# Sparse graph attention: when the neighbour rows of the first two lists of irregular rows are gathered, and when they are mixed

## The chip, the cores and the metric

The kernel runs on 1 core of one Trainium2 chip. The metric is device time in microseconds (us). Before the change three runs had a median of 823.53 us (822.4 to 824.62). A difference of about 0.3% (2.5 us) is the least that a measurement of this kernel can tell from none.

## The reference, cut to what matters

```python
h = jnp.maximum(_layernorm(x, axis=-1), 0.0)          # x: 8192 x 128
s_i = h @ attn[:d]; s_j = h @ attn[d:]
e = jax.nn.leaky_relu(s_i + s_j.T, negative_slope=0.2) # 8192 x 8192
e = e + jnp.where(adj > 0, 0.0, -1e9)                  # adj: 8192 x 8192 int32, 1 entry in 2048 set
out = x + jax.nn.softmax(e, axis=1) @ h
```

Each row of adj has some four neighbours on average. The kernel finds them and handles a row by its own few neighbours only.

## The kernel before, in words

adj is 8192 rows by 8192 int32, 268 MB, and all of it is read once. A tile is 128 rows (one in each partition); there are 64 tiles and so 32 pairs. One step p of 0 to 31 handles the pair of tiles 2p and 2p+1, in four halves of 128 x 4096 int32 (2 MB each):

- **SP** (the queue that loads and stores) issues the four halves of step p (`load_pair`, L413) into `adj_ring`, which has five places. A half may be issued when ACT has signed the half five before it. Between the loads of two steps SP stores a finished pair (`store_pair`, L418): after `load_pair(p)` it waits for the sum of pair p-4 (`pair_mixed`).
- **ACT** turns each half into signs (`sign_tile`, L610). In each step it also does a small exponential for a pair (`exp_pair`, L627, between the first two halves), and in the steps of `DEEP_MIX` one more, `exp_m` (L631), between the third and the fourth half.
- **PE** packs the signs into words (L1364) and collects irregular rows (`list_pair`, L1390).
- **DVE** takes maxima of the words (`max_tile`, L766), finds from them up to eight neighbour numbers of each row (`find_pair`, which ends in `near_id`, L818), scores the gathered neighbours of pair p-2 (`score_pair`, L903 to L919) and adds them up with their weights (L952).
- **POOL** gathers: 12 indirect DMAs for each pair (`gather_pair`, L518), each 128 rows of 528 bytes out of `h_table`. It waits for `near_id` of the pair.

Rows that don't fit that form are collected over the eight steps of a segment (`SEG` = 8) into a list of up to 128 rows; there are four lists, m = 0 to 3. List m is complete at step 8(m+1), where DVE finds 16 neighbour numbers for each of its rows (`find_deep`, which ends in `id_m`). POOL then gathers them with 16 indirect DMAs (`gather_m`, L529) and one for the rows of x (L534) into `near_m` and `x_m`, which have one copy each. `DEEP_PARTS` says how many of the 16 go behind the gathers of a pair in each step, and `DEEP_MIX` in which step of the segment the list is mixed: DVE waits for all 16 gathers (`score_deep`, L1015 to L1026), ACT does `exp_m`, DVE adds up (`add_deep`, to L1052), and POOL stores the result with an indirect DMA (`store_m`, L543), which stands ahead of that step's `gather_pair`. The last list is gathered and mixed behind the loop, and that is the same in both kernels.

The order on each engine is that of the code; nothing else reorders it. In the text S(p) is the time at which ACT starts to sign the first half of step p.

Of the kernel before, what the change touches and what calls it, by code (L numbers as in the profile page):

```python
# [5 lines left out]
def graph_attention_kernel(nc: bass.Bass, x: bass.AP, adj: bass.AP, attn: bass.AP, out: bass.AP):  # L6
# [46 lines left out]
    SEG = 8  # L53
# [3 lines left out]
    CLOSING = 3  # L57
    BODY = PAIRS - CLOSING

    DEEP_PARTS = (4, 4, 4, 4)  # L60
    DEEP_MIX = 6
    FAR = float(2 * N)
    MASKED = -1.0e9
    NOTHING = -1.0e30
# [36 lines left out]
    with ctx:  # L101
# [343 lines left out]
        def _(pool):  # L445
# [67 lines left out]
            def gather_pair(p):  # L513
                pool.wait_ge(near_id_ready, p + 1)
                if p >= RING:
                    pool.wait_ge(pair_mixed, p - RING + 1)
                for k in range(SLOTS):
                    pool.indirect_dma_start(  # L518
                        out=near[:, p % RING, k, :], out_offset=None, in_=table,
                        in_offset=bass.IndirectOffsetOnAxis(ap=near_id[:, p % IDS, k:k + 1], axis=0),  # L520
                        bounds_check=last_code, oob_is_err=False).then_inc(near_in[p % RING], 16)

            def gather_m(m, slots):
                if slots[0] == 0:
                    pool.wait_ge(id_m_ready, m + 1)
                    if m > 0:
                        pool.wait_ge(mixed_m_ready, m)
                for k in slots:
                    pool.indirect_dma_start(  # L529
                        out=near_m[:, k, :], out_offset=None, in_=table,  # L530
                        in_offset=bass.IndirectOffsetOnAxis(ap=id_m[:, k:k + 1], axis=0),
                        bounds_check=last_code, oob_is_err=False).then_inc(near_m_in, 16)
                if slots[-1] == DEEP - 1:
                    pool.indirect_dma_start(  # L534
                        out=x_m[:, :], out_offset=None, in_=x,
                        in_offset=bass.IndirectOffsetOnAxis(ap=row_m[:, m % 2:m % 2 + 1], axis=0),
                        bounds_check=last_row, oob_is_err=False).then_inc(x_m_in, 16)

            def store_m(m):
                pool.wait_ge(mixed_m_ready, m + 1)  # L540
                for e in range(2):
                    pool.wait_ge(stored[e], 16 * (m + 1) * SEG // 2)
                pool.indirect_dma_start(  # L543
                    out=out, out_offset=bass.IndirectOffsetOnAxis(ap=row_m[:, m % 2:m % 2 + 1], axis=0),
                    in_=mixed_m[:, 0, :], in_offset=None,
                    bounds_check=last_row, oob_is_err=False).then_inc(stored_m, 16)

            def load_lone(b):
                pool.wait_ge(lone_id_ready[b], 1)
                pool.indirect_dma_start(  # L550
                    out=lone_x[b], out_offset=None, in_=x,
                    in_offset=bass.IndirectOffsetOnAxis(ap=lone_id[b][:, 0:1], axis=0),
                    bounds_check=last_row, oob_is_err=False).then_inc(lone_x_in[b], 16)
# [8 lines left out]
                    bounds_check=last_row, oob_is_err=False).then_inc(lone_stored[b], 16)  # L562

            for p in range(PAIRS):
                if p >= SEG and p % SEG == DEEP_MIX:
                    store_m(p // SEG - 1)
                gather_pair(p)
                if p == FIRST_STEP + 2:
                    load_lone(0)
                m = p // SEG - 1  # L570
                if m >= 0 and p % SEG < len(DEEP_PARTS):
                    at = sum(DEEP_PARTS[:p % SEG])
                    gather_m(m, range(at, at + DEEP_PARTS[p % SEG]))
            gather_m(SEGS - 1, range(0, DEEP))
            load_lone(LAST)
            store_lone(0)
# [23 lines left out]
        def _(act):  # L600
            act.wait_ge(consts, 1)

            def sign_tile(t, halves=(0, 1)):
                for h in halves:
                    n = 2 * t + h
                    act.wait_ge(adj_in[n % HALVES], 16 * (n // HALVES) + 16)
                    if n >= 4:
                        act.wait_ge(packed, n - 3)
                    bytes_of = sign_ring[:, n % 4, :].rearrange("p (d i r) -> p d r i", d=DIGITS // 2, r=2)
                    nc.scalar.activation(bytes_of, adj_ring[:, n % HALVES, :].rearrange("p (d r i) -> p d r i", r=2, i=WORDS),  # L610
                                         ACT.Sign, bias=half_neg[:, :], saturate=False,
                                         accum_out=degree[:, t, h:h + 1]).then_inc(signed, 1)
# [16 lines left out]
            def exp_m(m):  # L629
                act.wait_ge(below_m_ready, m + 1)  # L630
                nc.scalar.activation(weight_m[:, :], below_m[:, :], ACT.Exp, accum_out=total_m[:, :]) \  # L631
                    .then_inc(weight_m_ready, 1)
# [35 lines left out]
            def exp_step(p):  # L668
                for g in MIXES.get(p, []):
                    exp_pair(g)  # L670
                for c in early_parts(p - 1 - FIRST_STEP):
                    exp_lone(0, c)

            for p in range(1, PAIRS):
                sign_tile(2 * p, (0,))
                exp_step(p - 1)
                sign_tile(2 * p, (1,))
                sign_tile(2 * p + 1, (0,))
                if p >= SEG and p % SEG == DEEP_MIX:
                    exp_m(p // SEG - 1)  # L680
                sign_tile(2 * p + 1, (1,))
            exp_step(PAIRS - 1)
# [30 lines left out]
        def _(dve):  # L713
# [46 lines left out]
            def max_tile(t):  # L760
                p = t // 2
                dve.wait_ge(packed, 2 * t + 2)
                if t % 2 == 0 and p >= 2:
                    dve.wait_ge(listed, p - 1)
                for q in range(QUARTERS):
                    last = nc.vector.max(out=cand[:, p % 2, t % 2, 8 * q:8 * q + 8],  # L766
                                         in_=words[t % 3][:, q * PART:(q + 1) * PART])
                last.then_inc(maxed, 1)
# [402 lines left out]
            def lone_begin(p):  # L1171
                if 0 <= p - FIRST_STEP - 3 < SUMS:
                    lone_add(p - FIRST_STEP - 3)
                if p == FIRST_STEP + 3 + SUMS - 1:
                    lone_end(0)

            def lone_step(p):
                if p == FIRST_STEP - 2:
                    lone_mark(0)
                if p == FIRST_STEP - 1:  # L1180
                    lone_compact(0)
                if p == FIRST_STEP:
                    lone_bounds(0)

            def lone_close(p):
                for c in early_parts(p - FIRST_STEP):
                    lone_part(0, c)
# [40 lines left out]
            for p in range(1, PAIRS):  # L1228
                mixes = MIXES.get(p, [])
                m = p // SEG - 1  # L1230
                lone_begin(p)
                max_tile(2 * p)
                if p in (1, PAIRS - 1):
                    key_pair(p - 1)
                if m >= 0 and p % SEG == DEEP_MIX:
                    score_deep(m)
                for g in mixes:
                    score_pair(g)
                if m >= 0 and p % SEG == DEEP_MIX:
                    add_deep(m)  # L1240
                max_tile(2 * p + 1)
                if 1 < p < PAIRS - 1:
                    key_pair(p - 1)
                find_pair(p)
                if p < PAIRS - 1:
                    for g in mixes:
                        weigh_mix(g)
                        add_pair(g, range(0, OWN))
                flag_pair(p)
                if m >= 0 and p % SEG == 0:  # L1250
                    find_deep(m)
                if p == PAIRS - 1:
                    lone_mark(LAST)
                    key_pair(p)
                    weigh_pair(BODY)
                    lone_compact(LAST)
                    score_pair(BODY + 1)
                    find_deep(SEGS - 1)
                    weigh_pair(BODY + 1)
                    mark_severe()  # L1260
                    lone_bounds(LAST)
                    size_loop()
                    dve.sem_inc(far_used, 1)
                    for c in range(LONE_PARTS[LAST]):
                        lone_part(LAST, c)
                    break
                lone_step(p)
                for g in mixes:
                    add_pair(g, range(OWN, 2 * OWN))
                lone_close(p)  # L1270
# [275 lines left out]
```

## Time and profile before

| | |
|---|---|
| median of 3 runs | 823.53 us (822.4 to 824.62) |
| profiled execution, its span | 872.6 us |
| instructions in it | 6682 |
| DVE busy | 551.5 us (63%) |
| ACT busy | 531.1 us (61%) |
| POOL busy | 511.4 us (59%) |
| PE busy | 375.1 us (43%) |
| DMA engines, mean busy share in slices 2 to 33 of 40 | nine tenths or more, with one slice at six tenths |

The page gives one execution under the profiler, whose span is 49 us longer than the median run. Busy times are sums over the span; the 40 slices of the page are 21.8 us each, so about one step each. A DMA share of 1.00 to 1.02 in a stretch is what the view shows when the 16 DMA engines have no gap. In a row of the timeline the first number is the start in us from the start of the span, the second the duration, and the bracket at the end is the idle time of the engine just before and what ended it.

### The profile page before, as it was taken

To read this page: it belongs to the slowest core of one execution; us is meant where nothing else is said; L and a number is where in the kernel's file an instruction comes from. 1 tells how busy PE (TensorE), PEld (TensorE's weight loads), DVE (VectorE), ACT (ScalarE), POOL (GpSimd) and SP (SyncE) were. 2 spreads that over 40 slices of the span, in tenths; PEclk is the share of its full clock that TensorE was granted. 3 is DMA by queue.
4 is the path that set the end of the run, shared out by engine and by line. 5 is a ranking of instruction groups with operands and counts; after the bars stand their busy time and mean duration, and the time that the engine had idled before them with its cause. 6 is when DMAs were issued, how large, how long until landed. Compare 5 with 4: busy or idle time off the path is not lost.

```text
span 872.6 us, 6682 instructions
## 1 busy us (share of the span) xinstructions
PE 375.1 (43%) x1359; PEld 170.1 (19%) x1378; DVE 551.5 (63%) x2318; ACT 531.1 (61%) x410; POOL 511.4 (59%) x526
## 2 busy tenths in 40 slices
PE   2625345334444343354434425344443456434255
PEld 1312011111111111111111101111121143323244
DVE  7897266757566562895736528876775964973231
ACT  5975576676666676486675729676666754721230
POOL 6812766746467767377573765774677473767500
PEclk9777555555555565555555655555555566676578
DMA  8999999999999999999999969999999998611100
GB/s 345 406 402 396 407 409 407 410 413 404 412 399 411 406 412 406 410 409 406 406 403 366 407 265 362 408 408 411 398 412 408 413 405 337 228 36 34 23 20 4
DMA packets 39721, 301.60 MB, mean 346 GB/s; under 512 B 10682, under 2 KB 17149, under 8 KB 22272
## 3 DMA queue, kind: packets, MB, share of 16 engines
q1 hardware_dynamic: 24032, 277.04, 78.6%
q0 software_dynamic: 15360, 23.88, 7.9%
q10 hardware_dynamic: 288, 0.26, 0.1%
q8 instruction: 11, 0.18, 0.1%
q14 instruction: 30, 0.25, 0.1%
HBM read 303.76 MB, written 8.98 MB: 358 GB/s over the span
## 4 chain that ended last, share of the span: by engine, by line
DVE 29%; issue 21%; DMA 21%; ACT 11%; another core or an unknown queue 10%; PE 4%; POOL 3%; SPq 0%; ACTq 0%; DVEq 0%; POOLq 0%
DMA adj_ring<-in_adj_dram 17%; ACT sign_ring L610 9%; DVE mixed L952 8%; DVE cand L766 3%; POOL near L518 3%; DVE near L752 2%; PE words L1440 2%; DMA h_table<-mixed 2%; DMA near<-h_table,near_id 2%; PE words L1404 1%; DVE one_hot L721 1%; DVE codes L783 1%; ACT h_all L622 1%; PE words L1364 1%
## 5 line engine op out<-in xcount | busy, mean ns | idle before, releaser
L610 ACT ACTIVATE sign_ring<-adj_ring,half_neg 128x4096 fp8e3<-128x4096 int32 x128 | 474.3, 3706 | 179.9 <-issue 83.1
L518 POOL DMA_INDIRECT near<-h_table,near_id x384 | 398.8, 1039 | 258.4 <-DVE near_id L818 129.6
L1364 PE MATMUL words<-sign_ring,pack_w 128*128 128x512 bf16 x511 | 220.8, 581 | 335.1 <-issue 202.5
L1364 PEld LDWEIGHTS words<-sign_ring,pack_w 128*128 128x128 bf16 x512 | 55.1, 126 | 497.5 <-issue 319.6
L952 DVE SCALAR_TENSOR_TENSOR mixed<-near,weight_n,mixed 128x128 f32<-128x128 f32 x406 | 116.8, 348 | 34.4 <-DVE mixed L952 23.7
L766 DVE MAX8 cand<-words 128x8 f32<-128x256 f32 x256 | 91.0, 419 | 54.4 <-issue 25.5
L529 POOL DMA_INDIRECT near_m<-h_table,id_m x64 | 64.1, 1002 | 19.5 <-issue 19.5
L1355 PE MATMUL words<-place,place_w 128*128 128x512 bf16 x110 | 55.6, 590 | 16.1 <-DVE key L858 11.2
L1390 PEld LDWEIGHTS listing<-cand,one_hot 128*128 128x128 f32 x128 | 32.9, 316 | 13.2 <-issue 9.6
L627 ACT ACTIVATE weight<-below 128x16 f32<-128x16 f32 x32 | 6.5, 203 | 47.2 <-DVE below L919 40.2
L1345 PE MATMUL listing<-h_all 128*1 128x128 f32 x128 | 19.9, 331 | 24.1 <-ACT h_all L622 24.1
L1390 PE MATMUL listing<-cand,one_hot 128*128 128x34 f32 x128 | 27.9, 358 | 1.9 <-issue 1.6
L1440 PE MATMUL rank<-h_all,x_all 128*64 128x129 f32 x128 | 21.2, 328 | 13.8 <-issue 10.4
L783 DVE TENSOR_TENSOR codes<-cand_i,code_mask 128x512 int32<-128x512 int32 x32 | 22.2, 692 | 7.2 <-remote 6.2
L1404 PE MATMUL words<-near,adj_ring 128*128 128x128 f32 x96 | 16.4, 339 | 22.3 <-ACT adj_ring L640 22.3
L610 ACT ACTIVATION_READ_ACCUMULATOR sign_ring<-adj_ring,half_neg 128x1 f32 x128 | 23.9, 187 | 0.0
L1382 PE MATMUL rank<-flag,before 128*128 128x2 bf16 x32 | 6.5, 202 | 38.9 <-DVE prior L852 21.8
L646 ACT ACTIVATE mixed<-words 128x256 f32<-128x256 f32 x3 | 1.1, 383 | 35.1 <-remote 32.7
L640 ACT ACTIVATE adj_ring<-ident,adj_ring 128x128 f32<-128x128 f32 x48 | 14.3, 387 | 13.4 <-issue 12.8
L1440 PEld LDWEIGHTS rank<-h_all,x_all 128*64 128x64 f32 x128 | 18.6, 169 | 15.9 <-issue 12.2
L952 DVE SCALAR_TENSOR_TENSOR mixed<-near,weight_n,x_all 128x128 f32<-128x128 f32 x58 | 17.8, 349 | 5.9 <-DVE weight_n L932 3.1
L752 DVE TENSOR_TENSOR near<-h_all,mixed 128x2048 f32<-128x2048 f32 x8 | 21.4, 2681 | 0.0
(271 smaller groups left out, 544.0 us busy)
## 6 DMA issues: line engine op xcount, KB each, us to landing
adj_ring<-in_adj_dram SPq DMA_DIRECT2D x128, 2048.0 KB
near<-h_table,near_id POOLq DMA_INDIRECT x384
h_table<-h_all POOLq DMA_DIRECT2D x4, 1056.0 KB, 15.7
x_all<-in_x_dram SPq DMA_DIRECT2D x4, 1024.0 KB, 9.4
out_dram<-mixed SPq DMA_DIRECT2D x30, 128.0 KB
near_m<-h_table,id_m POOLq DMA_INDIRECT x64
out_dram<-mixed ACTq DMA_DIRECT2D x2, 128.0 KB
adj_ring<-h_table SPq DMA_DIRECT2D x1, 132.0 KB, 2.6
```

The source lines that it names most:

```text
L518: pool.indirect_dma_start(out=near[:, p % RING, k, :], out_offset=None, in_=table, in_offset=bass.IndirectOffsetOnAxis(ap=near_id[:, p % I ...
L529: pool.indirect_dma_start(out=near_m[:, k, :], out_offset=None, in_=table, in_offset=bass.IndirectOffsetOnAxis(ap=id_m[:, k:k + 1], axis=0 ...
L610: nc.scalar.activation(bytes_of, adj_ring[:, n % HALVES, :].rearrange("p (d r i) -> p d r i", r=2, i=WORDS), ACT.Sign, bias=half_neg[:, :] ...
L752: nc.vector.tensor_tensor(prods, h_all[:, c * XT:(c + 1) * XT, 0:D], attn_b[:, a * D:(a + 1) * D].unsqueeze(1).broadcast_to([P, XT, D]), A ...
L766: last = nc.vector.max(out=cand[:, p % 2, t % 2, 8 * q:8 * q + 8], in_=words[t % 3][:, q * PART:(q + 1) * PART])
L783: nc.vector.tensor_tensor(codes[:, :, :, :].rearrange("p a w c -> p (a w) c"), cand_i[:, :, :].rearrange("p a w -> p (a w)").unsqueeze(2). ...
L952: ins = nc.vector.scalar_tensor_tensor(acc, near[:, e, slot, 0:D], weight_n[:, a * own + k:a * own + k + 1], base, ALU.mult, ALU.add)
L1355: nc.tensor.matmul(at[:, k * BANK:(k + 1) * BANK], place_w[:, :], place[:, k * BANK:(k + 1) * BANK], start=True, stop=False)
L1364: last = nc.tensor.matmul(at[:, k * BANK:(k + 1) * BANK], pack_w[:, d, :], twins[:, o + k * BANK:o + (k + 1) * BANK], start=False, stop=(d ...
L1390: last = nc.tensor.matmul(listing[:, 0:REC], one_hot[:, p % 2, a, :], cand[:, p % 2, a, :], start=(p % SEG == 0 and a == 0), stop=(p % SEG ...
L1404: last = nc.tensor.matmul(at, diagonal[:, i % 2, a * own + k, :], near[:, g % RING, slot, 0:D], start=False, stop=(k == own - 1))
L1440: last = nc.tensor.matmul(lone_sum[b], part[:, k * e:(k + 1) * e], h_all[:, c * lt + k, 0:ONE + 1], start=(first and k == 0), stop=(final ...
```

## The change

Two tables of numbers change, and the tests that read them. `DEEP_PARTS` becomes one tuple for each of the first three lists: the first two lists are gathered in seven steps of 2, 2, 2, 2, 2, 3 and 3 slots instead of four steps of 4; the third list stays as it was. `DEEP_MIX` becomes a list of steps: 15, 23 and 30 instead of 14, 22 and 30. The fetch of the rows of x goes with a list's last part, so it moves from steps 11 and 19 to steps 14 and 22.

```diff
-    DEEP_PARTS = (4, 4, 4, 4)
-    DEEP_MIX = 6
+    DEEP_PARTS = ((2, 2, 2, 2, 2, 3, 3), (2, 2, 2, 2, 2, 3, 3), (4, 4, 4, 4))
+    DEEP_MIX = [SEG * (m + 1) + at for m, at in enumerate((7, 7, 6))]
@@ POOL
-                if p >= SEG and p % SEG == DEEP_MIX:
+                if p in DEEP_MIX:
                     store_m(p // SEG - 1)
                 gather_pair(p)
...
-                if m >= 0 and p % SEG < len(DEEP_PARTS):
-                    at = sum(DEEP_PARTS[:p % SEG])
-                    gather_m(m, range(at, at + DEEP_PARTS[p % SEG]))
+                if m >= 0 and p % SEG < len(DEEP_PARTS[m]):
+                    at = sum(DEEP_PARTS[m][:p % SEG])
+                    gather_m(m, range(at, at + DEEP_PARTS[m][p % SEG]))
@@ ACT
-                if p >= SEG and p % SEG == DEEP_MIX:
+                if p in DEEP_MIX:
                     exp_m(p // SEG - 1)
@@ DVE
-                if m >= 0 and p % SEG == DEEP_MIX:
+                if p in DEEP_MIX:
                     score_deep(m)
                 for g in mixes:
                     score_pair(g)
-                if m >= 0 and p % SEG == DEEP_MIX:
+                if p in DEEP_MIX:
                     add_deep(m)
```

What POOL does for the first list, from step 10 on, `near` being the gathers of a pair and `near_m` those of the list; a row with x12 is one step. First before the change:

```order
L518 DMA near<-h_table,near_id 128x132 x12
L529 DMA near_m<-h_table,id_m 128x132 x4
L518 DMA near<-h_table,near_id 128x132 x12
L529 DMA near_m<-h_table,id_m 128x132 x4
L534 DMA x_m<-in_x_dram,row_m 128x128
L518 DMA near<-h_table,near_id 128x132 x24
L543 DMA out_dram<-mixed_m,row_m 8192x128
```

And after it, from step 12 on:

```order
L518 DMA near<-h_table,near_id 128x132 x12
L529 DMA near_m<-h_table,id_m 128x132 x2
L518 DMA near<-h_table,near_id 128x132 x12
L529 DMA near_m<-h_table,id_m 128x132 x3
L518 DMA near<-h_table,near_id 128x132 x12
L529 DMA near_m<-h_table,id_m 128x132 x3
L534 DMA x_m<-in_x_dram,row_m 128x128
L543 DMA out_dram<-mixed_m,row_m 8192x128
```

Before, the gathers of two pairs (steps 12 and 13) lie between the list's last gather and the store of its result; after, none does.

On ACT the exponential of the list (`weight_m`) is moved behind four more halves. Before the change, steps 13 to 15, a row with x4 being the last three halves of a step and the first of the next:

```order
L610 ACTIVATE sign_ring,degree<-adj_ring,half_neg 128x2x2x1024 x4
L627 ACTIVATE weight<-below 128x16
L610 ACTIVATE sign_ring,degree<-adj_ring,half_neg 128x2x2x1024 x2
L631 ACTIVATE weight_m,total_m<-below_m 128x16
L610 ACTIVATE sign_ring,degree<-adj_ring,half_neg 128x2x2x1024 x2
L627 ACTIVATE weight<-below 128x16
```

After it:

```order
L610 ACTIVATE sign_ring,degree<-adj_ring,half_neg 128x2x2x1024 x4
L627 ACTIVATE weight<-below 128x16
L610 ACTIVATE sign_ring,degree<-adj_ring,half_neg 128x2x2x1024 x4
L627 ACTIVATE weight<-below 128x16
L610 ACTIVATE sign_ring,degree<-adj_ring,half_neg 128x2x2x1024 x2
L631 ACTIVATE weight_m,total_m<-below_m 128x16
L610 ACTIVATE sign_ring,degree<-adj_ring,half_neg 128x2x2x1024 x2
```

The exponential keeps its place in the step, between the third and the fourth half, one step later. PE's and SP's orders are the same in both kernels.

## Rows read from the trace of the kernel before

**Rows 1.** The page: GB/s that the DMA engines moved, in 40 slices

```profile
GB/s 345 406 402 396 407 409 407 410 413 404 412 399 411 406 412 406 410 409 406 406 403 366 407 265 362 408 408 411 398 412 408 413 405 337 228 36 34 23 20 4
```

**Rows 2.** Stretches: start and end, length, busy times, PEclk, DMA share, GB/s

```profile
187.00:325.00 138.00, 58.74 (x156) 19.40 (x156) 87.88 (x402) 93.03 (x55) 83.94 (x84) 0.52 1.01 408
...
338.60:365.00 26.40, 11.42 (x30) 3.72 (x30) 15.77 (x73) 15.20 (x9) 9.99 (x10) 0.50 1.01 407
...
452.50:480.00 27.50, 10.83 (x29) 3.58 (x30) 14.13 (x67) 16.47 (x10) 11.67 (x12) 0.52 0.94 372
...
714.60:748.00 33.40, 18.55 (x79) 9.18 (x80) 18.59 (x71) 12.26 (x9) 15.76 (x17) 0.70 0.90 353
...
497.30:533.00 35.70, 10.33 (x27) 3.54 (x29) 16.67 (x72) 15.80 (x10) 19.40 (x20) 0.50 0.77 299
```

**Rows 3.** SP's timeline: the loads of adj on both sides of four pauses

```profile
338.61 0.33 SPq L413 DMA_DIRECT2D adj_ring<-in_adj_dram  x1
...
353.77 0.42 SPq L413 DMA_DIRECT2D adj_ring<-in_adj_dram  x1
...
452.52 0.33 SPq L413 DMA_DIRECT2D adj_ring<-in_adj_dram  x1
...
468.95 0.43 SPq L413 DMA_DIRECT2D adj_ring<-in_adj_dram  x1
...
497.29 0.33 SPq L413 DMA_DIRECT2D adj_ring<-in_adj_dram  x1
...
523.66 0.43 SPq L413 DMA_DIRECT2D adj_ring<-in_adj_dram  x1
...
714.65 0.33 SPq L413 DMA_DIRECT2D adj_ring<-in_adj_dram  x1
...
734.85 0.33 SPq L413 DMA_DIRECT2D adj_ring<-in_adj_dram  x1
```

**Rows 4.** Waits of SP's queue: us in total, times, longest

```profile
SPq L418 <- DVE mixed L952: 117.9, 13, 25.6
```

**Rows 5.** ACT's timeline: first and third half of step 7, first half of step 13

```profile
187.39 3.71 ACT L610 ACTIVATE sign_ring<-adj_ring,half_neg 128x4096 fp8e3<-128x4096 int32 x1 [2.35 <-DMA adj_ring<-in_adj_dram]
...
197.88 3.71 ACT L610 ACTIVATE sign_ring<-adj_ring,half_neg 128x4096 fp8e3<-128x4096 int32 x1 [1.62 <-DMA adj_ring<-in_adj_dram]
...
323.83 3.71 ACT L610 ACTIVATE sign_ring<-adj_ring,half_neg 128x4096 fp8e3<-128x4096 int32 x1 [1.92 <-issue]
```

**Rows 6.** DVE's timeline: neighbour numbers of pair 7, first maxima of step 8

```profile
214.28 0.17 DVE L818 TENSOR_TENSOR near_id<-offset,unused 128x12 int32<-128x12 f32 x1
...
221.54 0.76 DVE L766 MAX8 cand<-words 128x8 f32<-128x256 f32 x2 [0.89 <-issue]
```

**Rows 7.** POOL's timeline: first gather of pair 7; first and last of step 8

```profile
214.72 0.99 POOL L518 DMA_INDIRECT near<-h_table,near_id  x1 [4.33 <-DVE near_id L818]
...
238.11 0.99 POOL L518 DMA_INDIRECT near<-h_table,near_id  x1 [8.01 <-DVE near_id L818]
...
257.71 0.99 POOL L529 DMA_INDIRECT near_m<-h_table,id_m  x1 [0.30 <-issue]
```

**Rows 8.** The chain that ended last: gathers, from issue to landing

```profile
97.33 6.85 DMA near<-h_table,near_id
...
132.74 6.37 DMA near<-h_table,near_id
```

**Rows 9.** The mix of list 0 in step 14, on DVE and on ACT

```profile
368.55 0.37 DVE L1015 TENSOR_SCALAR score_m<-near_m,si_m 128x16 f32<-128x16 f32 x1
...
369.84 0.22 ACT L631 ACTIVATE weight_m<-below_m 128x16 f32<-128x16 f32 x1 [6.31 <-issue]
...
375.95 0.29 DVE L1052 TENSOR_TENSOR mixed_m<-mixed_m 128x128 f32<-128x128 f32 x1
```

**Rows 10.** DVE's timeline in step 17: additions of pair 15

```profile
446.82 0.35 DVE L952 SCALAR_TENSOR_TENSOR mixed<-near,weight_n,mixed 128x128 f32<-128x128 f32 x1
448.41 0.35 DVE L952 SCALAR_TENSOR_TENSOR mixed<-near,weight_n,mixed 128x128 f32<-128x128 f32 x1 [1.24 <-DVE mixed L952]
```

## The prediction

> **What bounds the kernel now.** Read the page's row of GB/s first [rows 1]: from the second slice to the 33rd the DMA engines move about 400 to 413 GB/s, save in slices 22, 24 and 25 (366, 265 and 362). The stretches say the same as a share: from 187 to 325 us it is 1.01, no gap at all [rows 2]. So the loop runs at the pace at which adj arrives. ACT signs the first half of step 7 at 187.39 and that of step 13 at 323.83 [rows 5], so a step is 136.44 / 6 = 22.7 us, and before each half ACT has sat idle for 1.6 to 2.4 us. DVE, ACT and POOL are busy for less than that in a step (87.88, 93.03 and 83.94 us in 138 [rows 2], about 14 to 15 us of 22.7), so their work costs nothing by itself. What costs is a wait that keeps SP from issuing the next half for so long that the ring's five places run dry.
>
> That happens, and the trace has four pauses of SP from which a price can be read [rows 3]. The loss of a stretch is its length times what its DMA share lacks to 1.01 [rows 2]:
>
> - 338.61 to 353.77, a pause of 15.2 us: share 1.01, loss 0
> - 452.52 to 468.95, 16.4 us: 27.5 x 0.07 = 1.9 us
> - 714.65 to 734.85, 20.2 us: 33.4 x 0.11 = 3.7 us
> - 497.29 to 523.66, 26.4 us: 35.7 x 0.24 = 8.6 us
>
> So up to some 15 us of pause are free, and beyond 20 each further us costs nearly one ((8.6 - 3.7) / (26.4 - 20.2) = 0.8). Three of the four end with SP's wait for a pair that DVE has to finish (117.9 us over 13 waits in all [rows 4]).
>
> **What the change takes away: nothing on the path.** In steps 8 to 11 and 16 to 19 POOL issues 14 gathers instead of 16, and the three steps behind each, which had 12, now have 14 or 15. A gather starts every (257.71 - 238.11) / 15 = 1.31 us [rows 7], so a step of POOL takes 18.3 us instead of 20.9. Both are under the 22.7 us of a step: after 16 as after 14 gathers POOL waits for `near_id`. The work hidden behind the adj stream stays hidden; the relief is worth 0. If POOL were the pace in those eight steps it would be worth up to 8 x 2.6 = 21 us, but then the DMA share would not be 1.01 there. The bytes are the same. In steps 14 and 22 DVE loses the list's mix, from 368.55 to 376.2, 7.7 us less 1.3 for the pair's scores that lie between [rows 9]; it is hidden in both places, and so worth 0 again. ACT's wait of 6.31 us there [rows 9] goes too. It cost nothing: the DMA share of the stretch around it holds at 1.01 [rows 2].
>
> **What it adds: a wait of DVE and ACT for the list's last gathers.** Before, these were issued three steps ahead of the mix. Now they are issued behind the 12 gathers of pair 14, and DVE asks for them after its first maxima of step 15. Count from S(14), with the offsets of a step that waited only for adj:
>
> - `near_id` of the pair: 214.28 - 187.39 = 26.9 us after S [rows 5, 6]
> - POOL's first gather 0.4 us later (214.72) [rows 7]
> - the 15th gather (12 of the pair, 3 of the list) starts 14 x 1.31 = 18.3 us later, at 45.6
> - it lands 6.85 or 6.37 us after its issue [rows 8]; I take 6.6: 52.2 us
> - from `score_m` to `exp_m` 369.84 - 368.55 = 1.3 us [rows 9]: 53.5 us, that is S(15) + 30.8
>
> DVE wants those rows at about 221.54 + 1.4 - 187.39 = 35.6 us [rows 5, 6], so it stands for 16.6 us. Behind the waiting instruction are queued the scores of pair 13, the second maxima and `near_id` of pair 15, for which POOL waits, and the sum of pair 13, for which SP waits. ACT is what hurts first. It has signed the third half of step 15 at 197.88 - 187.39 + 3.8 = 14.3 us after S(15) [rows 5] and then stands in `exp_m` until 30.8, so for 16.5 us, of which some 2 were idle anyway. The fourth half is signed at 30.8 + 0.2 + 3.8 = 34.8. Since a place in the ring comes free only when a half is signed, SP's pause is 34.8 - 14.3 = 20.5 us, where it is 22.7 / 4 = 5.7 else. By the 20.2 us pause a pause of 20.5 costs about 3.8 us, and there are two (lists 0 and 1; list 2 keeps its place): 7.5 us. I take 7, since the third half's sign can come a little later than in step 7.
>
> **What follows the wait.** DVE's work from the mix to the end of step 15 is all late by some 17 us and then runs without waits. Its 14 us of work in a step against 22.7 take that back in two to three steps. SP asks for the sum of pair 13 ahead of step 18's loads, about two steps later, when the DVE is already nearly in time: 0 as the likeliest, and it is rival 3 if it isn't. POOL's store of the list now waits for `mixed_m` in step 15, with `gather_pair(15)` behind it; that one waits for `near_id` of pair 15 anyway, which DVE makes later than `mixed_m`, so this wait adds 0. Its step is 12 to 14 gathers, 16 to 18 us, so it recovers 4 to 7 us a step too.
>
> **A price that the notes give.** The trace shows 6.4 to 6.9 us from the issue of one gather to its landing under a full adj stream [rows 8]. The Trainium skill (DMA: Bandwidth & Descriptors, section on the anatomy of one DMA, SWDGE path) fits a DMA from GpSimd at 2.0 us plus bytes over 436 GB/s, which for 67.6 KB is 2.2 us. By that the wait would end 4.4 us earlier, the pause would be 16.1 us and the two losses together about 3 us; the rows are of this load, so the sum goes by them.
>
> **The sum.** Against the profiled execution: 872.6 + 7 = 879.6 us. The median of the runs is 49 us shorter than that span; the halves arrive as fast or faster there, so the wait in us stays and I add the same 7 us: 823.5 + 7 = 830.5 us, 0.85% slower. Bounds of the terms: the landing 6.4 to 6.9; the offset of `near_id` 26.9 in a step on time and 35 in step 14 of this trace, where DVE was late (near 26.9, since in step 14 the mix itself is now gone); the loss of a pause of 20.5 us from 2 (the row at 16.4) to 9 (the row at 26.4). That makes 3 to 18 us for both, 826 to 841.
>
> **Rival 1, the ring covers it.** If without the profiler POOL's gathers run a little faster or land sooner, the pause falls to 15 to 17 us and costs 0 to 1 us each. Time 823 to 826. For it: the pause of 15.2 us was free, and 5 us are not much in a chain of 53. Against it: 15 gathers at 1.31 us are simple issue and vary little. Chance 0.27.
>
> **Rival 2, faster.** DVE has spells in which it sits idle between two instructions of which each needs only the one before: an addition of 0.35 us starts at 446.82 and the next at 448.41, with 1.24 us idle between them [rows 10]. In steps 17 and 19 such spells hold up the sums that SP waits for, and the losses of 1.9 and 8.6 us follow. Both start while POOL issues 16 gathers of a step and goes on to the next without a pause. If back-to-back gathers cause the spells, 14 instead of 16 leave POOL a pause in each step, the spells go, and 10.5 us come back, while the ring covers most of the new wait: 823.5 - 10.5 + 2 = 815 us. It decides if POOL's 16 gathers hold DVE. Against it: in steps 8 and 9 POOL issues as many, and DVE is on time; the spells also come in steps with 12; and they may belong to the profiler. Chance 0.24.
>
> **Rival 3, much slower.** The new lateness of 17 us meets a spell like that of step 17, of about 20 us. DVE is then 37 us late. On time it ends a step some 34 us after S (221.54 - 187.39 [rows 5, 6]), and SP asks for that pair at two steps, 45.5 us; with the 15 us of pause that are free, 26 us of lateness cost nothing. The other 11 do, some 10 us for each list: 843 us. For it: before the change the mix of 7.7 us in step 14 was followed by two losses. Chance 0.13.
>
> **Chances.** The forecast (over 826 to 836) 0.36, rival 3 0.13, rival 1 0.27, rival 2 0.24. So slower by over 0.3% (2.5 us, about what a measurement can tell) 0.49, within it 0.27, faster 0.24. With one tenth left out at either side the range is 815 to 842; the likeliest case alone has 826 to 836.
>
> **What would show it.** In the changed kernel's trace: DVE idle for 14 to 19 us ahead of L1015 in steps 15 and 23, ended by the gather; ACT idle for about as long ahead of L631; a pause of SP's loads of about 20 us there, and a DMA share under 1.01 in the stretch behind it; POOL waiting for `near_id` in each of steps 8 to 13. If the pause is there with the DMA share at 1.01, rival 1 holds. If the spells on DVE in steps 16 to 20 are gone, rival 2 does. The forecast is wrong if the landing is much faster than 6 us or if what bounds the unprofiled run is not the adj stream.

## The result, and the profile after

The changed kernel's median is 825.93 us (824.13 to 828.59, 12 runs) beside 824.49 us (822.4 to 826.18, 12 runs) of the kernel before. The ratio is 1.0027, with a 95% interval of 1.0017 to 1.0037: 0.27% slower, 2.2 us by the ratio and 1.4 by the medians, which is just within the 0.3% that the prediction called the same. The forecast had been 7 us slower, 0.85%. Two later comparisons of the same kernel gave 0.9999 (0.999 to 1.0007) and 1.0011 (1.0002 to 1.002), so by the runs the difference is 0 to 2 us.

One thing has to be said of the profile that stood ahead of the prediction: it was of an execution 50 us longer than all others of either kernel. Profiled again (the first experiment below) the kernel before has a span of 817.6 us, and what differs is named there.

The page of after, its span, and GB/s in 40 slices of 20.6 us:

```profile
span 825.5 us, 6701 instructions
...
GB/s 345 401 406 424 389 404 407 411 405 411 407 402 404 409 414 400 404 408 406 331 395 405 403 412 410 408 406 409 360 401 405 407 406 407 408 412 81 50 38 6
```

Against [rows 1] the dips of slices 22, 24 and 25 are gone, and there are two others, 331 in slice 20 and 360 in slice 29. They are the pauses of steps 15 and 23. The places of step 15 on each engine, in the timelines of after: DVE's neighbour numbers of pair 14 and its first work on the list, with the idle time ahead of it; POOL's last gather of the list; ACT's third half, its `exp_m`, and the fourth half; SP's loads on both sides.

```profile
374.00 0.17 DVE L818 TENSOR_TENSOR near_id<-offset,unused 128x12 int32<-128x12 f32 x1
...
398.86 0.23 DVE L1015 TENSOR_SCALAR score_m<-near_m,si_m 128x16 f32<-128x16 f32 x1 [16.63 <-DMA near_m<-h_table,id_m]
```

```profile
392.73 1.00 POOL L529 DMA_INDIRECT near_m<-h_table,id_m  x1 [0.30 <-issue]
```

```profile
379.05 3.71 ACT L610 ACTIVATE sign_ring<-adj_ring,half_neg 128x4096 fp8e3<-128x4096 int32 x1 [0.99 <-DMA adj_ring<-in_adj_dram]
...
400.02 0.22 ACT L631 ACTIVATE weight_m<-below_m 128x16 f32<-128x16 f32 x1 [17.17 <-DVE below_m L1026]
...
400.23 3.69 ACT L610 ACTIVATE sign_ring<-adj_ring,half_neg 128x4096 fp8e3<-128x4096 int32 x1
```

```profile
382.87 0.33 SPq L413 DMA_DIRECT2D adj_ring<-in_adj_dram  x1
...
404.04 0.33 SPq L413 DMA_DIRECT2D adj_ring<-in_adj_dram  x1
...
566.60 0.33 SPq L413 DMA_DIRECT2D adj_ring<-in_adj_dram  x1
...
585.88 4.02 SPq L413 DMA_DIRECT2D adj_ring<-in_adj_dram  x2
```

The reader sees the predicted chain, step for step: the last gather is issued at 392.73, the rows are there at 398.86, DVE has stood for 16.6 us, ACT for 17.2, and SP's pauses are 404.04 - 382.87 = 21.2 us in step 15 and 585.88 - 566.60 = 19.3 in step 23. What is not there is the predicted loss of 7 us. The two stretches around the pauses lack 27 x 0.13 + 28 x 0.06 = 5.2 us of DMA share against 1.01 (start and end, length, busy times, PEclk, DMA share, GB/s):

```profile
385.00:412.00 27.00, 5.12 (x14) 1.38 (x15) 12.49 (x60) 11.98 (x10) 9.18 (x10) 0.50 0.88 346
566.00:594.00 28.00, 6.32 (x18) 1.79 (x19) 12.65 (x60) 12.73 (x12) 9.71 (x11) 0.56 0.95 376
```

### The profile page after: what moved, and what is told of

It reads as the page before. It is cut to its first block, busy times and chain, and to the rows that moved or that the text cites. A ratio compares the mean times of both kernels' runs of the same rounds, so it can differ in the third digit from the quotient of the medians.

```text
span 825.5 us, 6701 instructions
## 1 busy us (share of the span) xinstructions
PE 375.4 (45%) x1378; PEld 168.8 (20%) x1378; DVE 547.6 (66%) x2318; ACT 532.5 (64%) x410; POOL 504.2 (61%) x526
## 4 chain that ended last, share of the span: by engine, by line
DMA 60%; issue 13%; DVE 11%; ACT 7%; POOL 4%; PE 4%; SPq 0%; DVEq 0%; ACTq 0%; POOLq 0%
DMA adj_ring<-in_adj_dram 53%; ACT sign_ring L610 6%; POOL near L518 4%; DVE near L752 3%; DMA out_dram<-mixed 2%; PE words L1440 2%; DMA h_table<-mixed 2%; DMA near_m<-h_table,id_m 1%; DVE one_hot L721 1%; DMA near<-h_table,near_id 1%; ACT h_all L622 1%; PE words L1364 1%; PE words L1404 1%; DMA x_all<-in_x_dram 1%; DVE h_all L757 1%
## 5 line engine op out<-in xcount | busy, mean ns | idle before, releaser
L518 POOL DMA_INDIRECT near<-h_table,near_id x384 | 391.8, 1020 | 225.3 <-issue 124.2
L952 DVE SCALAR_TENSOR_TENSOR mixed<-near,weight_n,mixed 128x128 f32<-128x128 f32 x406 | 111.4, 345 | 0.0
L1355 PE MATMUL words<-place,place_w 128*128 128x512 bf16 x128 | 61.2, 578 | 1.5 <-DVE key L858 1.5
L1440 PEld LDWEIGHTS rank<-h_all,x_all 128*64 128x64 f32 x128 | 20.8, 185 | 4.9 <-DVE key L858 4.9
L903 DVE TENSOR_SCALAR score<-near,h_all 128x8 f32<-128x8 f32 x32 | 7.9, 247 | 20.4 <-DMA near<-h_table,near_id 20.4
L543 POOL DMA_INDIRECT out_dram<-mixed_m,row_m x4 | 4.1, 1016 | 27.3 <-DVE mixed_m L1052 14.4
L495 POOL TENSOR_SCALAR h_all<-x_all,codes 128x128 f32<-128x128 f32 x16 | 13.0, 829 | 11.7 <-DVE codes L738 11.7
## 6 DMA issues: line engine op xcount, KB each, us to landing
adj_ring<-in_adj_dram SPq DMA_DIRECT2D x128, 2048.0 KB, 24.6
```

The costliest lines, as they stand in the source:

```text
L518: pool.indirect_dma_start(out=near[:, p % RING, k, :], out_offset=None, in_=table, in_offset=bass.IndirectOffsetOnAxis(ap=near_id[:, p % I ...
L952: ins = nc.vector.scalar_tensor_tensor(acc, near[:, e, slot, 0:D], weight_n[:, a * own + k:a * own + k + 1], base, ALU.mult, ALU.add)
L1355: nc.tensor.matmul(at[:, k * BANK:(k + 1) * BANK], place_w[:, :], place[:, k * BANK:(k + 1) * BANK], start=True, stop=False)
L1440: last = nc.tensor.matmul(lone_sum[b], part[:, k * e:(k + 1) * e], h_all[:, c * lt + k, 0:ONE + 1], start=(first and k == 0), stop=(final ...
```

## The experiments

### The kernel before, profiled again

No edit.

> The kernel before, profiled once more, unchanged. The profile of before had a span of 872.6 us against a median of 823.5, with spells on DVE in which each instruction took 0.7 us or a multiple of it; the profile of after has a span of 825.5 and no such spell. Theory A (the spells were an accident of that one execution): the span is 822 to 826 us, no pause of SP's loads over 12 us behind step 2 is longer than the ring covers, and the DMA share of the loop is 1.00 or 1.01 in steps 12 to 29. Theory B (the spells belong to the kernel before and the new spreading of the gathers took them away): span again over 850 us with losses in steps 17 to 22.

Measured: 819.36 us, beside a median of 820.01 us over 29 runs of the kernel before. Theory A holds, though the span of 817.6 us is 4 us shorter than it gave. The row of GB/s has no dip from the second slice to the 35th, and behind the first few loads no pause of SP is over 12.2 us:

```profile
GB/s 346 422 419 429 402 406 405 408 413 414 415 414 407 407 408 408 406 415 410 413 413 409 408 407 408 411 409 410 415 413 405 411 408 408 403 311 44 50 39 6
```

So the spells of DVE [rows 10], the two losses in steps 17 to 21 and much of the 872.6 us belonged to that one execution, and rival 2, which was built on them, had nothing to take away. A third execution (the run `e11_before_third`) says the same, with a span of 820.0 us and no pause over 11.0 us from step 4 on.

This trace also shows what the end of the adj stream looks like when nothing disturbs it. SP issues the last half at 721.30, and ACT, waiting for it, signs it at 745.99:

```profile
721.30 0.33 SPq L413 DMA_DIRECT2D adj_ring<-in_adj_dram  x1
```

```profile
745.99 3.71 ACT L610 ACTIVATE sign_ring<-adj_ring,half_neg 128x4096 fp8e3<-128x4096 int32 x1 [1.64 <-DMA adj_ring<-in_adj_dram]
```

In between, by stretches:

```profile
722.00:728.00 6.00, 1.42 (x5) 0.43 (x4) 5.30 (x22) 3.80 (x2) 5.07 (x4) 0.57 1.00 404
728.00:731.00 3.00, 1.46 (x7) 0.89 (x6) 2.08 (x9) 2.16 (x1) 2.02 (x2) 0.50 0.87 339
731.00:734.00 3.00, 3.00 (x16) 3.00 (x15) 2.83 (x16) 1.75 (x3) 0.00 (x0) 0.50 0.18 63
734.00:746.00 12.00, 7.96 (x38) 4.86 (x37) 9.74 (x45) 7.61 (x5) 9.11 (x9) 0.78 0.20 62
```

The share falls from 1.00 to 0.18 at 731, yet the last half lands 15 us later. The packets of adj tell why: summed over each microsecond from 733 to 744, those of 8 KB and more keep 0.8 to 1.0 engine busy (1.9 in one of these microseconds), where it is about 15 before 728, and from 734 to 741 no two of them overlap. Fifteen engines have done their part of everything that was issued, and one still works alone; a half has landed when the last engine is done with it. So the pace of the loop is that of one DMA engine of 16, and the others run ahead of it; how far ahead they are is called their lead below. The third execution ends in the same way, as was expected of it: the share is 0.20 from 734 to 746 us, and the last half, issued at 722.50, is signed at 747.11, 24.6 us later.

### A pause of the same origin, four ways

These runs take the cost apart: the wait with ACT placed otherwise, and the later mix and the spreading without the wait. First, `exp_m` behind the fourth half and not ahead of it, for lists 0 and 1:

```diff
-                if p in DEEP_MIX:
+                late = p in DEEP_MIX[:2]
+                if p in DEEP_MIX and not late:
                     exp_m(p // SEG - 1)
                 sign_tile(2 * p + 1, (1,))
+                if late:
+                    exp_m(p // SEG - 1)
```

> The changed kernel, but in steps 15 and 23 ACT does exp_m behind the fourth half and not ahead of it. Theory A (what costs is the pause of SP's loads of 21.2 and 19.3 us that ACT's wait in exp_m makes): ACT signs one half more before it stands, the pause shrinks by 5.7 us to 14 to 16 us, the DMA share stays at 1.01, and the kernel is 2 to 5 us faster than after: 821 to 824 us, ratio to before 0.996 to 1.000. Theory B (the cost is DVE's lateness of 17 us, which stays as it is): no gain over after, ratio 1.002 to 1.004.

Measured: 820.92 us, ratio 1.0009 (1.0 to 1.0018). The pauses are 15.3 and 13.9 us, as A has it, but the DMA share is 0.99 and 0.94 and not A's 1.01. The time is not told apart from that of the changed kernel, whose ratio in a later comparison on the same chip is 0.9999 (below). So it decides nothing in time: there was hardly anything to win.

Then `exp_m` behind the first half of the next step:

```diff
                 sign_tile(2 * p, (0,))
+                if p - 1 in DEEP_MIX[:2]:
+                    exp_m((p - 1) // SEG - 1)
                 exp_step(p - 1)
...
-                if p in DEEP_MIX:
+                if p in DEEP_MIX[2:]:
                     exp_m(p // SEG - 1)
```

> The changed kernel, but ACT does exp_m of lists 0 and 1 behind the first half of the next step (16 and 24), two halves later than in after. DVE still waits for the list's last gathers, as long as in after. Theory A (the cost is the pause that ACT's wait makes): the pause falls to 8 to 10 us, no DMA is missing there, and the ratio is 0.999 to 1.001. Theory B (DVE's lateness costs by itself): ratio 1.002 or more, as after.

Measured: 820.22 us, ratio 0.9995 (0.9986 to 1.0003). DVE idles as before, 16.4 and 15.7 us ahead of its scores of the list, but ACT's wait is short, and the DMA share is full:

```profile
395.72 0.22 ACT L631 ACTIVATE weight_m<-below_m 128x16 f32<-128x16 f32 x1 [4.27 <-DVE below_m L1028]
```

```profile
385.00:412.00 27.00, 11.44 (x34) 3.60 (x32) 16.56 (x78) 18.98 (x12) 9.19 (x10) 0.56 1.01 420
566.00:594.00 28.00, 12.54 (x36) 3.92 (x37) 17.46 (x81) 19.94 (x15) 9.47 (x10) 0.56 1.01 412
```

DVE's lateness of 16 us costs nothing by itself: that part of the prediction stands. The trace agrees: from S(15) to S(23) it takes 181.8 us, as the kernel before does in its second and third traces, where the changed kernel takes 182.4 to 183.5. The missing share comes from ACT's wait alone.

The later mix alone, the gathers in four steps as before:

```diff
-    DEEP_PARTS = ((2, 2, 2, 2, 2, 3, 3), (2, 2, 2, 2, 2, 3, 3), (4, 4, 4, 4))
+    DEEP_PARTS = ((4, 4, 4, 4), (4, 4, 4, 4), (4, 4, 4, 4))
```

> The change's later mix alone: lists 0 and 1 are mixed in steps 15 and 23 as in after, and gathered in four steps of 4 slots as before. The rows have landed three steps ahead, so DVE and ACT don't wait for them. Theory A (the whole cost of the change is that wait): same as before, ratio 0.999 to 1.001. Theory B (mixing later costs by itself, for instance by the store of the list or by DVE's work next to find_deep): ratio 1.001 to 1.004. If it is under 0.999, the change had a gain in the later mix that the wait used up.

Measured: 820.43 us, ratio 0.9996 (0.9988 to 1.0005), DVE with no idle time ahead of the list. The later mix costs nothing and brings nothing.

The spreading without the wait, in six steps, mixed in steps 15 and 23, measured twice:

```diff
-    DEEP_PARTS = ((2, 2, 2, 2, 2, 3, 3), (2, 2, 2, 2, 2, 3, 3), (4, 4, 4, 4))
+    DEEP_PARTS = ((3, 3, 3, 3, 2, 2), (3, 3, 3, 3, 2, 2), (4, 4, 4, 4))
```

> Lists 0 and 1 are gathered in six steps of 3, 3, 3, 3, 2, 2 slots and mixed in steps 15 and 23: the last gather is issued a step and a half before the mix, so the spreading is there without the wait. Theory A (spreading is worth nothing by itself): as the kernel with the later mix alone, 0.999 to 1.001. Theory B (POOL's relief is worth something, which would explain why after lost only 1.4 to 2.2 us where its profile shows 4.8 us of missing DMA): ratio 0.995 to 0.998, and below the kernel with the later mix alone.

Measured: 819.21 us, ratio 0.999 (0.9981 to 1.0).

> The spreading over six steps of 3, 3, 3, 3, 2, 2 slots with the mix in steps 15 and 23 once more, which came out at 0.999 (0.9981 to 1.0). Theory A (nothing on the path is touched): 0.999 to 1.001. Theory B (a small gain): 0.997 to 0.9995 again.

Measured: 821.65 us, ratio 0.9997 (0.9988 to 1.0006). The first looked like a small gain, and the second doesn't bear it out. POOL's relief is worth nothing that can be measured, as predicted. No version here beats the kernel before.

### The change for list 0 alone

```diff
-    DEEP_PARTS = ((2, 2, 2, 2, 2, 3, 3), (2, 2, 2, 2, 2, 3, 3), (4, 4, 4, 4))
-    DEEP_MIX = [SEG * (m + 1) + at for m, at in enumerate((7, 7, 6))]
+    DEEP_PARTS = ((2, 2, 2, 2, 2, 3, 3), (4, 4, 4, 4), (4, 4, 4, 4))
+    DEEP_MIX = [SEG * (m + 1) + at for m, at in enumerate((7, 6, 6))]
```

> The change made for list 0 alone: seven steps and the mix in step 15; list 1 is gathered and mixed as before. Theory A (two like losses): half of after's difference, ratio 1.000 to 1.002, one pause of about 20 us in step 15 and none in steps 22 or 23. Theory B (one of the two lists does all the harm): either as after or as before.

Measured: 821.06 us, ratio 1.0007 (0.9997 to 1.0017), one pause of 20.8 us. It is as expected, but since the full change came out at 0.9999 beside the same runs of the kernel before it can't tell a half from a whole.

### The changed kernel again, and with a longer wait

The changed kernel was measured twice more, each time beside the kernel before; the second of these comparisons was on another chip.

> The changed kernel unchanged, on the chip and beside the runs of the three others of this call. Its one profile shows 4.8 us of missing DMA behind its two pauses, while the runs differ by 1.4 us in the medians and 2.2 in the ratio. Theory A (each execution loses 3 to 5 us, and the profile of after fell on one of the slower): pauses of 18 to 20 us, ratio 1.002 to 1.004. Theory B (the missing DMA time is made up elsewhere, by a gain of the later mix or of the spreading): the profile shows again 4 to 5 us missing and a ratio of 1.000 to 1.003.

Measured: 820.13 us beside 820.42, ratio 0.9999 (0.999 to 1.0007). The pauses are 20.8 and 19.6 us, and the two stretches lack 27 x 0.18 + 28 x 0.09 = 7.4 us of share:

```profile
385.00:412.00 27.00, 8.18 (x25) 3.08 (x26) 16.42 (x78) 16.15 (x12) 9.21 (x10) 0.56 0.83 330
...
566.00:594.00 28.00, 9.54 (x26) 3.28 (x26) 16.92 (x79) 16.65 (x12) 9.73 (x10) 0.50 0.92 370
```

So 7.4 us of DMA share are missing, more than either theory gave, and the median is the same. The ratio is as B had it, but not for B's reason, since neither the later mix nor the spreading gains anything. The finer stretches of the first pause show the reason, together with the stream's end in the same trace:

```profile
397.00:400.00 3.00, 0.10 (x1) 0.10 (x2) 2.93 (x14) 3.00 (x3) 0.00 (x0) 0.50 0.09 34
...
728.00:740.00 12.00, 8.31 (x44) 5.98 (x43) 9.67 (x47) 7.62 (x5) 6.26 (x7) 0.74 0.99 403
740.00:747.00 7.00, 4.29 (x16) 1.83 (x16) 4.98 (x23) 3.93 (x5) 5.41 (x6) 0.57 0.27 80
```

From 397 to 400 the share is 0.09, which is 1.4 engines of 16: the slowest goes on while the others stand, and the next half is issued at 399.88, before it is through. What the 15 others have lost is mostly their lead. By the packets more than half of the engines stand from 395.6 us, and the last load issued has landed at 403.2: a lead of 7.5 us in step 15, where it is about 15 at the end of an undisturbed stream. At the end of this trace the 15 are busy until 740 and not 731, and the last half is signed at 746.97. In the kernel before the same idle time of the 15 stands at the end of the stream; the change moves it into the middle. What the pauses did cost in this trace is read below, from S(15) on: 1.6 us of the 7.4.

> The changed kernel unchanged, a third time, since its ratio was 1.0027 in the first comparison and 0.9999 in the second. Theory A (its pauses lie at the edge of what is free, and the small difference goes with the chip or the hour): anything from 0.999 to 1.004, pauses of 19 to 21.5 us. Theory B (one of the two comparisons was off and the change is worth the same everywhere): 1.001 to 1.002.

Measured: 822.9 us beside 821.96, ratio 1.0011 (1.0002 to 1.002), pauses of 20.9 and 19.2 us, 7.4 us of share missing again. That is within A's bounds, and B's 1.001 to 1.002 is not excluded either. The missing share and the measured cost are not tied to each other: 5.2 us missing with 2.2 us lost in the first profile, 7.4 with 0, 7.4 with 0.9.

Then the wait made longer, by putting more of the list into the last step. Two gathers more:

```diff
-    DEEP_PARTS = ((2, 2, 2, 2, 2, 3, 3), (2, 2, 2, 2, 2, 3, 3), (4, 4, 4, 4))
+    DEEP_PARTS = ((2, 2, 2, 2, 2, 1, 5), (2, 2, 2, 2, 2, 1, 5), (4, 4, 4, 4))
```

> The changed kernel with 2, 2, 2, 2, 2, 1 and 5 slots for lists 0 and 1: the list's last gather two gathers, 2.6 us, later than in after. Theory A (the pause costs only what it is longer than the time for which the slowest DMA engine still has work, about 22 us from the last issue): pauses of 23.4 and 22.2 us, lost 1 us at the first and 0 to 1 at the second, ratio 1.000 to 1.003. Theory B (what is lost is the mean share of the 16 engines that is missing, as the prediction read it): some 11 us missing in the two stretches and lost, ratio 1.010 or more.

Measured: 826.18 us beside 821.96, ratio 1.0052 (1.0036 to 1.0067), pauses of 23.3 and 22.2 us. The time lies between the two theories. The missing share is 27 x 0.26 + 31 x 0.12 = 10.7 us, and 4.3 us are lost, so B is refuted; but A's 1 to 2 us are too few as well, if they are to be the whole loss.

```profile
385.00:412.00 27.00, 4.75 (x13) 1.29 (x14) 12.18 (x58) 11.61 (x10) 9.18 (x10) 0.50 0.75 294
566.00:597.00 31.00, 7.85 (x22) 2.43 (x20) 13.98 (x65) 13.51 (x10) 11.98 (x13) 0.50 0.89 356
```

Four gathers more:

```diff
-    DEEP_PARTS = ((2, 2, 2, 2, 2, 3, 3), (2, 2, 2, 2, 2, 3, 3), (4, 4, 4, 4))
+    DEEP_PARTS = ((2, 2, 2, 1, 1, 1, 7), (2, 2, 2, 1, 1, 1, 7), (4, 4, 4, 4))
```

> The changed kernel with 2, 2, 2, 1, 1, 1 and 7 slots for lists 0 and 1: the list's last gather is issued four gathers later, 4 x 1.31 = 5.2 us. Theory A (beyond the pause that the ring covers each us costs nearly one): the pauses grow from about 20 to 25 us, some 5 us more are lost at each, together 8 to 10 us beyond after, ratio 1.012 to 1.016. Theory B (the rest of the kernel makes up for most of it): ratio under 1.008.

Measured: 827.86 us beside 820.42, ratio 1.0087 (1.0074 to 1.01), pauses of 25.7 and 24.8 us. Here the slowest engine runs dry too. SP's pause, and the stretches in it and around both pauses:

```profile
379.43 0.33 SPq L413 DMA_DIRECT2D adj_ring<-in_adj_dram  x1
...
405.16 0.33 SPq L413 DMA_DIRECT2D adj_ring<-in_adj_dram  x1
```

```profile
400.00:403.00 3.00, 0.00 (x0) 0.00 (x0) 2.65 (x16) 1.87 (x3) 0.00 (x0) 0.50 0.07 29
403.40:406.00 2.60, 0.81 (x2) 0.28 (x3) 2.60 (x12) 2.60 (x3) 0.00 (x0) 0.50 0.01 2
385.00:412.00 27.00, 4.68 (x12) 1.22 (x12) 11.47 (x53) 10.87 (x8) 10.11 (x11) 0.50 0.66 259
571.00:597.00 26.00, 4.69 (x12) 1.23 (x12) 11.13 (x48) 10.42 (x8) 9.14 (x10) 0.50 0.78 307
```

Until 403 one engine works (0.07 x 16 = 1.1), from 403.4 to 406 none does (0.01). That is 24 us after the last issue, and a new half starts to move about 1 us after it is issued, so the first pause idles the slowest engine for some 3 us. Missing share 27 x 0.35 + 26 x 0.23 = 15.4 us, lost 7.1 us. The ratio lies between the two theories: less is lost than A's 8 to 10 us beyond the changed kernel.

The loss can also be read inside each trace, from S(15) to the first sign of the last half. For the kernel before (its second trace) and the changed kernel (its second):

```profile
365.43 3.71 ACT L610 ACTIVATE sign_ring<-adj_ring,half_neg 128x4096 fp8e3<-128x4096 int32 x1 [1.87 <-DMA adj_ring<-in_adj_dram]
```

```profile
364.74 3.71 ACT L610 ACTIVATE sign_ring<-adj_ring,half_neg 128x4096 fp8e3<-128x4096 int32 x1 [2.00 <-DMA adj_ring<-in_adj_dram]
...
746.97 3.71 ACT L610 ACTIVATE sign_ring<-adj_ring,half_neg 128x4096 fp8e3<-128x4096 int32 x1 [1.61 <-DMA adj_ring<-in_adj_dram]
```

That is 745.99 - 365.43 = 380.56 us and 746.97 - 364.74 = 382.23. The five traces without a wait for the list (the kernel before twice, the later mix alone, the six steps twice) have 380.5 to 380.7, so this measure is far steadier than the span. What it leaves out is large: at S(4), before anything that the change touches, the thirteen traces other than the first already differ by 3.7 us (114.7 to 118.4).

All of it together, in us for both pauses, the last column against 380.6:

| kernel | pauses | share missing | lost, from the ratio | lost, in the trace |
|---|---|---|---|---|
| changed, three comparisons | 19.2 to 21.2 | 5.2, 7.4, 7.4 | 2.2, 0, 0.9 | 3.2, 1.6, 2.9 |
| five in the last step | 23.3, 22.2 | 10.7 | 4.3 | 4.6 |
| seven in the last step | 25.7, 24.8 | 15.4 | 7.1 | 8.7 |

A pause of 20 us costs 0 to 1 us by the runs and 0.8 to 1.6 in the traces, and beyond it each further us costs about (7.1 - 1.0) / (50.5 - 40.3) = 0.6, by the traces too. What comes beyond the changed kernel is, with seven slots, mostly the time in which the slowest engine stands as well. By the packets no engine moves adj for 2.8 and 2.7 us in the two pauses of the seven-slot kernel, which loses 6.1 us more than the changed kernel's mean of 2.6, and for 0.5 and 0.4 us in the five-slot one, which loses 2.0 more.

## Why the prediction was wrong

**What bounds the kernel:** half right. The loop goes at the pace of the adj stream; but a DMA share of 1.01 was read as if all 16 engines were the bound. It is one of them.

**What the change takes away, nothing on the path:** right. The later mix alone gave 0.9996 and the spreading without the wait 0.999 and 0.9997. Before the change DVE never waited for a list's gathers in the loop.

**What it adds:** right in every link, and close in size. Predicted were 16.6 us of DVE, 16.5 of ACT and a pause of 20.5; measured in step 15 of after 16.6, 17.2 and 21.2, in step 23 15.3, 15.3 and 19.3. The landing of the last gather was taken at 6.6 us; it is 398.86 - 392.73 = 6.1. The Trainium skill's fit (DMA: Bandwidth & Descriptors, section on the anatomy of one DMA, SWDGE path) gave an estimate of 2.2 us for such a DMA. Under the full adj stream the same rows refute it; behind the stream it is close, for in the second trace of the kernel before the 16 gathers of the last list, from 765 to 800 us, land 2.5 us after their issue in the median:

```profile
near_m<-h_table,id_m POOLq DMA_INDIRECT x16, 2.5
```

**The price of a pause: this is the step that failed.** "By the 20.2 us pause a pause of 20.5 costs about 3.8 us". It was read as the length of a stretch times the DMA share that it lacks [rows 2]. Such a stretch did lack 3.5 us in after and 4.9 in the second profile, so the reading was right as a reading. For the most part it was no loss of time. The mean over 16 engines counts the 15 that stand, and these are ahead by up to 15 us anyhow (they are done at 731 of 746 when the stream ends undisturbed). Instead of 3.8 us a pause of this length costs 0 to 1.1 by the runs and 0.8 to 1.6 in the traces, and both together 0 to 2.2 or 1.6 to 3.2 instead of 7. The fall of the GB/s at the end of [rows 1] was no warning, since in that trace the engines finish within a few us of each other (share 0.97 from 750 to 753 us, 0.17 from 756 to 760). A finer stretch inside its longest pause would have been one, as the next paragraph shows.

**The rows of the pauses** were besides of the one disturbed execution. In it the stretch of the 26.4 us pause was priced at 8.6 us; in it, too, part is the 15 engines' idle time, as its own trace shows. One engine works from 517 to 520 (0.08) and none from 521 to 524:

```profile
517.00:520.00 3.00, 0.67 (x2) 0.00 (x0) 0.91 (x3) 0.00 (x0) 2.19 (x2) 0.50 0.08 28
521.00:524.00 3.00, 0.00 (x0) 0.00 (x0) 2.46 (x10) 0.00 (x0) 0.00 (x0) 0.50 0.00 0
```

**The rivals.** Rival 1, that the ring covers it, is what happened, at 823 to 826 us, with a chance of 0.27; but by another way than it gave, so that its figure was right by luck. It wanted the pause to shrink to 15 to 17 us, and the pause stayed at 20. Rival 2 is out: the spells were not POOL's doing, since the kernel before shows none in its two other traces. Rival 3 did not occur; DVE's lateness by itself cost nothing even with the wait at full length.

**What stays open.** The idle time of the slowest engine explains 5.5 of the 6.1 us that the seven-slot kernel loses beyond the changed one, and 0.9 of the 2.0 of the five-slot one. Why a pause of 15 to 21 us costs some 1 us before that engine runs dry was not settled; the kernel with `exp_m` behind the fourth half, whose pauses are 15.3 and 13.9 us, still loses 1.5 us by its trace (382.1 against 380.6 us). Why the same kernel differs from before by 2.2 us in one comparison and by 0 in another was not settled either; in single traces a spread of 3.7 us is there at S(4). Which engine is the slow one and why, these views don't show. The Trainium skill (DMA: Bandwidth & Descriptors, section on latency and other measured facts) says that two of the engines, numbers 7 and 15, are usually slower than the rest, and guesses at the descriptor rings of GpSimd's DMAs as the cause; the trace agrees in part, since it shows one slow engine and not two, and no run here took the gathers away to test the cause.

## What to carry to other kernels

A DMA share that falls is not yet a loss: ask when the transfer that is waited for lands, and compare the landings of the two kernels, counted from a common point ahead of the change, not the gap in the mean over 16 engines. Price a stall from how late the next work starts, and only from an execution whose span agrees with the unprofiled runs; an execution 50 us longer than the median is to be distrusted for sizes, even where its order of events is sound. And an instruction that may wait long should stand where the engine's other work doesn't queue behind it: behind the first half of the next step, `exp_m` left the DMA engines fully busy where before it stopped them.

## What the runs showed of the hardware that was not expected

One DMA engine of 16 sets the pace of a stream of 2 MB loads, each spread over all of them. With five loads in flight the other 15 finish their parts of the last ones some 12 to 15 us ahead of it (731 against 746 us), where in step 15 their lead was 7.5 us, while a load takes 24.7 us from issue to landing. And one execution under the profiler had DVE start dependent instructions 0.7 us or a multiple of it apart for stretches of 20 us, which none of the other thirteen traces shows; it was 50 us longer.
